# Moving the low parts of two weight sets from VectorE to GpSimd in a two-layer transformer kernel

## The chip, the cores and the metric

The kernel runs on one core of a Trainium2 chip. The metric is the device time of one execution in microseconds, as the median of several runs. The core's engines run side by side, each with an instruction stream of its own, and wait for each other by semaphores: TensorE (PE in the profile), VectorE (DVE), ScalarE (ACT), GpSimd (POOL) and SyncE (SP), which issues the transfers.

## What is computed

The input is x of 8 sequences x 512 rows x 256 columns. Two layers follow each other:

```python
xn = _layernorm(x)
x = x + _L0_attn_ref(xn, Wq, bq, Wk, bk, Wv, bv, Wo, bo)   # 16 heads of 64, rotary, causal softmax
      + _L0_ffn_ref(xn, weight_int8, weight_scale, bias)   # rows quantised to int8 by one scale
xn = _layernorm(x)
x = x + _L1_attn_ref(xn, compare_left, compare_right, threshold, gate_bias)
      + _L1_ffn_ref(xn, W_r, W_k, W_v, mu_r, mu_k)
```

The matrix products are to be nearly as precise as float32 ones, while TensorE multiplies float16. So each weight matrix is scaled by a power of two and split in a high part (float16 of the scaled weight) and a low part (float16 of what the high part leaves), and each product is made of three: high x high, high x low, low x high.

## The kernel before, in words

**Stages.** A short set-up loads x and the query and key weights and makes their high and low parts. The first layer, some 50 to 830 us of the span, handles 64 pairs of heads (8 sequences x 8 pairs). The second layer follows, one pass of `body3` per sequence.

**The passes.** Each engine has its own function `ring(n)`, called for n = -5 to 62. Pass n finishes pair n, computes scores and softmax of pair n+1 and projects queries and keys of phase n+5 (a phase is the queries or the keys of two pairs). Nothing is scheduled at run time: the order of the calls inside each `ring(n)` is the order in which that engine works, and each call waits for what it needs. The order around the change:

- TensorE: scores of (n+1, 0); `v(n)`; transposes `pt(n, j, h)` (L1773) of the probabilities of pair n, which for j = 0 wait until GpSimd has normalised them; from pass 10 on also the output projection `attended` (L1804) and the quantised layer `ffn`; `evens(n+5)`; scores of (n+1, 1); `odds(n+5)`; last `av(n)` (L1787).
- ScalarE: exponentials `exps(n+1, 0)` and, later in the pass, `exps(n+1, 1)` (L890), with copies and the high halves `high_e`, `high_o` of the rotated phase n+4 between them. `later_weights(n)` comes after all of them. It makes the high parts of the output weights, two quarters in pass 7 and two in pass 8 (L852, semaphore `wo_hi`), and those of the five matrices of the second layer in passes 24 to 28 (L808, `wr_hi`).
- VectorE: maxima of the scores of (n+1, 0) in three parts with `out_low(n-1)` (L1405) and `first_gap(n)` after the first; `second_gap(n)`; `even_terms(n+5)`; `inverse(n+1, 0)` (L1391), the reciprocals of the softmax sums; maxima of (n+1, 1); `odd_terms(n+5)`; `inverse(n+1, 1)`; `ring_end(n)`, in which `quantise` has its steps (L1415 to L1426).
- GpSimd: `normalise(n, 1)` (L646, four instructions, waits for `inverse(n, 1)`); `rotate(n+4)` (L618, L620); `low_e(n+4)` (L628), `low_o(n+4)` (L636), which wait for ScalarE's high halves; in some passes `add_bias` (L655); `normalise(n+1, 0)`; in some passes `add_ffn` (L662).

**Low parts.** VectorE makes each with one instruction, `scalar_tensor_tensor`: staged weight times `inv`, minus the high part. For the output weights (4 quarters of 128 x 512) that is `low_part(c)` in `ring_end` of passes 7, 8 and 10 (L1271). For the second layer (two of 128 x 256, three of 128 x 512) it is `weights_low` (L1219) in `first_gap` of passes 25 to 29.

**Who reads them.** `attended(0, 0, ...)` waits for `wo_lo` in passes 10 and 11. SyncE waits for `wo_lo` 4 before it loads the second layer's weights over the staged output weights. The second layer's products wait for `wr_lo` 5 after the last pass.

**Small steps.** The scales of the second layer's weights come from maxima over the whole matrices. `column_maximum` is in `first_gap(20)`; `weight_scale` (L1211 to L1213, three linked instructions of 1 to 5 columns) is in `second_gap(20)`, and three pairs of instructions on one to four columns (L1310 to L1318) are in `second_gap` of passes 21 to 23.

Of the kernel before, what the change touches and what calls it, by code (L numbers as in the profile page):

```python
# [6 lines left out]
SQ = 512  # L7
D = 256
# [19 lines left out]
NG = 9  # L28
# [15 lines left out]
def build(nc, x_d, weights_d, w8_d, bqk_d, vec_d, thr_d, gate_d, tab_d, out_d):  # L44
# [11 lines left out]
    with ctx:  # L56
# [205 lines left out]
        wr_hi = sem("wr_hi")  # L262
        wr_lo = sem("wr_lo")
        w8_done = sem("w8_done")
        xm_done = sem("xm_done")
# [315 lines left out]
        def _(pool):  # L581
# [75 lines left out]
            def add_ffn(b, h):  # L657
# [4 lines left out]
                pool.tensor_tensor(tiles, tiles, fft.rearrange("p (t d) -> p t d", t=2), ALU.add).then_inc(fx_done, 1)  # L662

            def ring(n):

# [5 lines left out]
                if b >= 0 and r % 4 == 1:  # L671
                    add_bias(b, r // 4)
                if n == NR - 2:
                    for h in range(2):
                        add_bias(NB - 1, h)
# [415 lines left out]
        def _(dve):  # L1091
# [174 lines left out]

            def low_part(c):

                part = slice(c * SQ, (c + 1) * SQ)
                dve.wait_ge(wo_hi, c + 1)  # L1270
                dve.scalar_tensor_tensor(out=wl[:, C_O:C_LR][:, part], in0=wst_r[:, part], scalar=inv[:, G_O:G_O + 1],  # L1271
                                         in1=wh[:, C_O:C_LR][:, part], op0=ALU.mult, op1=ALU.subtract).then_inc(wo_lo, 1)

            def part_maximum(c):
# [5 lines left out]
            def first_gap(n):  # L1280

                if n == 0:
                    roots(later_tiles, 1, (1, 2), wo)
                elif n == NB - 1:
                    dve.wait_ge(amax_done, NB)
                    dve.tensor_reduce(xmax1[:], amax[:], AX.X, ALU.max).then_inc(xm_done, 1)
                elif n == 20:
                    column_maximum(slice(G_L, NG), 4)
                elif 25 <= n < 25 + NG - G_L:
                    weights_low(G_L + n - 25, (wr_hi, n - 24), wr_lo)  # L1290

            def second_gap(n):
# [8 lines left out]
                elif 13 <= n < 17:  # L1301
# [3 lines left out]
                    else:  # L1305
                        weight_maximum(slice(G_WR + n - 14, G_WR + n - 13))
                elif n == 20:
                    weight_scale(slice(G_L, NG), 4)
                elif n == 21:
                    dve.scalar_tensor_tensor(out=sc_c[:], in0=sc[:, G_L:G_L + 1], scalar=D ** -0.5, in1=sc[:, G_R:G_R + 1],  # L1310
                                             op0=ALU.mult, op1=ALU.mult)
                    dve.tensor_scalar(sc_hr[:], sc[:, G_WR:G_WR + 1], 0.5, None, ALU.mult)
                elif n == 22:
                    link(dset, dve.tensor_tensor(thr_c[:], inv[:, G_L:G_L + 1], inv[:, G_R:G_R + 1], ALU.mult))
                    dve.scalar_tensor_tensor(out=thr_c[:], in0=thr_c[:], scalar=D ** 0.5, in1=thr[:], op0=ALU.mult, op1=ALU.mult)
                elif n == 23:
                    dve.tensor_scalar(sc_hv[:], sc[:, G_WV:G_WV + 1], 0.5, None, ALU.mult)
                    dve.tensor_scalar(omu[:], vec[:, V_MUR:V_MUR + 4], -1.0, 1.0, ALU.mult, ALU.add)  # L1318
                elif NR - 6 <= n <= NR - 3:
# [4 lines left out]
            def ring_end(n):  # L1324
# [3 lines left out]
                if n == 7:  # L1328
                    quantise(0, 0)
                    low_part(0)  # L1330
                elif n == 8:
                    input_scale()
                    low_part(1)
                elif n == 9:
                    for step in range(1, 4):
                        quantise(0, step)
                elif n == 10:
                    low_part(2)
                    low_part(3)

# [771 lines left out]
```

## Time and profile before

| | before |
|---|---|
| median of 3 runs | 1019.11 us (1018.42 to 1019.32) |
| the profiled execution | 1019.33 us, its span 1017.4 us |
| TensorE busy | 975.8 us (96%) |
| VectorE busy | 839.6 us (83%) |
| ScalarE busy | 746.0 us (73%) |
| GpSimd busy | 764.1 us (75%) |

The profile shows one execution. A line of the timeline gives the start in us, the time in us (of x instructions together, where it ends in a count), the engine, the line of the program, the operation, the tiles written and read, and in brackets how long the engine was idle before it and who ended that. A custom or pipelined instruction's end is modelled, so starts are surer than durations.

### The profile page before, as it was taken

To read this page: it belongs to the slowest core of one execution; us is meant where nothing else is said; L and a number is where in the kernel's file an instruction comes from. 1 tells how busy PE (TensorE), PEld (TensorE's weight loads), DVE (VectorE), ACT (ScalarE), POOL (GpSimd) and SP (SyncE) were. 2 spreads that over 40 slices of the span, in tenths; PEclk is the share of its full clock that TensorE was granted. 3 is DMA by queue.
4 is the path that set the end of the run, shared out by engine and by line. 5 is a ranking of instruction groups with operands and counts; after the bars stand their busy time and mean duration, and the time that the engine had idled before them with its cause. 6 is when DMAs were issued, how large, how long until landed. Compare 5 with 4: busy or idle time off the path is not lost.

```text
span 1017.4 us, 23654 instructions
## 1 busy us (share of the span) xinstructions
PE 975.8 (96%) x7956; PEld 673.2 (66%) x7956; DVE 839.6 (83%) x2272; ACT 746.0 (73%) x1998; POOL 764.1 (75%) x942
## 2 busy tenths in 40 slices
PE   5789999999999999999999999999999998989998
PEld 4556665766666666666666666666666675766776
DVE  7989999788889888887788777877878778999885
ACT  5989987667766677666767766667666776988984
POOL 3777768778778787878787878787878665878885
PEclk9999999999999999999999999999999999999999
DMA  8733535243433333333333333333333101111111
GB/s 271 242 111 119 155 121 160 79 131 112 124 111 93 105 106 94 95 114 96 93 95 119 96 103 97 116 97 100 105 96 95 53 1 27 35 35 35 48 55 43
DMA packets 102903, 101.32 MB, mean 100 GB/s; under 512 B 13952, under 2 KB 98560, under 8 KB 102144
## 3 DMA queue, kind: packets, MB, share of 16 engines
q1 hardware_dynamic: 102784, 99.81, 32.2%
q8 instruction: 65, 1.06, 0.5%
q14 instruction: 54, 0.44, 0.2%
HBM read 56.25 MB, written 40.90 MB: 95 GB/s over the span
## 4 chain that ended last, share of the span: by engine, by line
PE 70%; DVE 16%; ACT 4%; POOL 4%; issue 3%; DMA 2%; SPq 0%; DVEq 0%; POOLq 0%; ACTq 0%
PE bank L1690 23%; PE bank L1787 13%; PE bank L1773 12%; PE bank L1804 8%; PE bank L1761 6%; PE bank L1762 5%; DVE arena L1382 2%; POOL arena L646 2%; PE bank L1931 2%; DVE arena L1398 2%; ACT arena L890 1%; PE bank L1991 1%; DVE arena L1550 1%; DVE arena L1360 1%; DMA arena<-in_weights 1%
## 5 line engine op out<-in xcount | busy, mean ns | idle before, releaser
L646 POOL TENSOR_SCALAR arena<-arena,rc 128x128 f32<-128x128 f32 (+3 forms) x512 | 278.0, 560 | 176.5 <-DVE rc L1391 176.2
L890 ACT ACTIVATE arena<-arena,nm 128x256 f32<-128x256 f32 (+3 forms) x512 | 283.5, 554 | 109.0 <-DVE nm L1382 104.4
L1382 DVE CUSTOM_DVE_ANT_0 arena<-bank,mask_rows 128x256 f32<-128x256 f32 (+3 forms) x512 | 232.9, 483 | 89.0 <-PE bank L1762 83.9
L1773 PE MATMUL bank<-ident,arena 128*128 128x128 f32 x1280 | 211.8, 278 | 9.5 <-DVE arena L1398 4.4
L1773 PEld LDWEIGHTS bank<-ident,arena 128*128 128x128 f32 x1280 | 150.0, 141 | 68.4 <-DVE arena L1398 29.3
L1762 PE MATMUL bank<-arena 128*128 128x256 f16 (+3 forms) x512 | 152.9, 299 | 0.0
L1787 PE MATMUL bank<-arena 128*64 128x512 f32 (+3 forms) x1024 | 152.0, 439 | 0.0
L1761 PE MATMUL bank<-arena 128*128 128x256 f16 (+3 forms) x512 | 139.9, 300 | 2.0 <-DMA arena<-scr 2.0
L1787 PEld LDWEIGHTS bank<-arena 128*64 128x64 f32 x1024 | 67.8, 136 | 95.1 <-issue 70.6
L1398 DVE COPY arena<-bank 128x512 f32<-128x512 f32 (+3 forms) x256 | 124.5, 486 | 3.3 <-PE bank L1773 2.9
L898 ACT ACTIVATE arena<-bank 128x512 f32<-128x512 f32 (+3 forms) x256 | 108.3, 423 | 15.0 <-PE bank L1773 14.2
L1690 PE MATMUL bank<-xsh,wh 128*128 128x512 f16 x256 | 97.3, 380 | 3.1 <-DVE wl L1228 2.4
L1804 PE MATMUL bank<-wh,arena 128*128 128x256 f16 x512 | 99.7, 273 | 0.0
L1690 PE MATMUL bank<-xsl,wh 128*128 128x512 f16 x256 | 97.3, 380 | 0.0
L1690 PE MATMUL bank<-xsh,wl 128*128 128x512 f16 x256 | 97.3, 380 | 0.0
L890 ACT ACTIVATION_READ_ACCUMULATOR arena<-arena,nm 128x1 f32 x512 | 96.0, 187 | 0.0
L908 ACT ACTIVATE arena<-bank,bvs 128x512 f16<-128x512 f32 x64 | 44.0, 687 | 69.8 <-PE bank L1787 69.5
L1690 PE MATMUL bank<-wh,xsh 128*128 128x128 f16 x512 | 89.1, 219 | 1.6 <-DVE arena L1373 1.6
L1690 PE MATMUL bank<-wl,xsh 128*128 128x128 f16 x512 | 89.1, 219 | 0.0
L1690 PE MATMUL bank<-wh,xsl 128*128 128x128 f16 x512 | 89.1, 219 | 0.0
L618 POOL TENSOR_TENSOR arena<-arena 128x512 f32<-128x512 f32 x64 | 81.5, 1274 | 6.6 <-DVE arena L1373 6.5
L620 POOL TENSOR_TENSOR arena<-arena 128x512 f32<-128x512 f32 x64 | 83.0, 1296 | 0.0
(183 smaller groups left out, 2164.2 us busy)
## 6 DMA issues: line engine op xcount, KB each, us to landing
arena<-scr SPq DMA_DIRECT2D x320, 128.0 KB, 2.7
scr<-arena SPq DMA_DIRECT2D x256, 128.0 KB, 1.7
arena<-in_weights SPq DMA_DIRECT2D x5, 1024.0 KB, 7.5
x_sb<-in_x SPq DMA_DIRECT2D x8, 512.0 KB, 8.7
out<-x_sb SPq DMA_DIRECT2D x16, 256.0 KB, 2.2
xscr<-arena SPq DMA_DIRECT2D x12, 256.0 KB, 3.0
arena<-wh SPq DMA_DIRECT2D x40, 64.0 KB, 2.0
xsh<-xscr SPq DMA_DIRECT2D x6, 256.0 KB, 3.5
```

The lines of the kernel that those rows point to most:

```text
L620: pool.tensor_tensor(r_o, t_es, t_oc, ALU.add).then_inc(r1_done, 1)
L646: last = pool.tensor_scalar(pr[slot][:, OFF[i]:OFF[i + 1]], pr[slot][:, OFF[i]:OFF[i + 1]], rc[:, slot, i:i + 1], 1.0, ALU.mult, ALU.mult)
L890: act.activation(pr[slot][:, OFF[i]:OFF[i + 1]], pr[slot][:, OFF[i]:OFF[i + 1]], ACT.Exp, scale=-1.0, bias=nm[:, slot, i:i + 1], accum_out ...
L898: act.activation(ptf[h][:, TOFF[j]:TOFF[j + 1]], (pt0, pt1)[h][:, 0:P * (NT - j)], ACT.Copy).then_inc(ptf_done[h], 1)
L1382: dve.tensor_tensor_reduce(pr[slot][:, OFF[i]:OFF[i + 1]], s_tile[i], mask_rows[:, SQ - P * (i + 1):SQ], -1.0, -MASKED, ALU.add, ALU.min, ...
L1398: dve.tensor_copy(ptf[1][:, TOFF[j]:TOFF[j + 1]], pt1[:, 0:P * (NT - j)]).then_inc(ptf_done[1], 1)
L1690: last = pe.matmul(out, lhs, rhs, start=(a == 0), stop=(a == len(pairs) - 1))
L1761: pe.matmul(out, q, kd[par][:, hh, 0:(i + 1) * P], start=True, stop=False)
L1762: last = pe.matmul(out, q, kz[par][:, hh, 0:(i + 1) * P], start=False, stop=True)
L1773: last = pe.transpose(banks[5 + h][:, (i - j) * P:(i - j + 1) * P], pr[2 * par + h][:, OFF[i] + j * P:OFF[i] + (j + 1) * P], ident[:])
L1787: last = pe.matmul(ob[h * L:(h + 1) * L, j * P:SQ], vf[:, j, h * L:(h + 1) * L], ptf[h][:, TOFF[j]:TOFF[j + 1]], start=(j == 0), stop=(j = ...
L1804: last = pe.matmul(bank[:, t * D:(t + 1) * D], o[:, slot, rows], w[:, p, :], start=(p == 0 and a == 0 and t == 0), stop=(p == NP - 1 and a ...
```

## The change

The low parts move to GpSimd. There each takes two instructions: the staged weights are scaled in place, and behind a semaphore of their own the high part is subtracted. `later_low(n)` does it in `ring(n)` between `low_o`/`add_bias` and `normalise(n+1, 0)`: the output weights' four quarters in passes 7, 8, 9, 10, the second layer's five matrices in passes 26, 27, 28, 30, 31. VectorE's `low_part` and its part of `first_gap` go. Its small steps move from `second_gap` of passes 20 to 23 to `first_gap` of passes 21 to 24.

```diff
+            def low_part(w, staging, g, turn, high, done):
+                pool.wait_ge(*high)
+                pool.tensor_scalar(staging, staging, inv[:, g:g + 1], 1.0, ALU.mult, ALU.mult).then_inc(wst_scaled, 1)
+                pool.wait_ge(wst_scaled, turn + 1)
+                pool.tensor_tensor(w[1], staging, w[0], ALU.subtract).then_inc(done, 1)
+            def later_low(n):
+                if 7 <= n < 11:
+                    c = n - 7
+                    part = slice(c * SQ, (c + 1) * SQ)
+                    low_part([w[:, C_O:C_LR][:, part] for w in (wh, wl)], wst_r[:, part], G_O, c, (wo_hi, c + 1), wo_lo)
+                elif n in (26, 27, 28, 30, 31):
+                    c = (26, 27, 28, 30, 31).index(n)
+                    g = G_L + c
+                    low_part([wgroup(w, g) for w in (wh, wl)], staged(g), g, 4 + c, (wr_hi, c + 1), wr_lo)
...
                 if b >= 0 and r % 4 == 1:
                     add_bias(b, r // 4)
+                later_low(n)
...
-            def low_part(c):
-                part = slice(c * SQ, (c + 1) * SQ)
-                dve.wait_ge(wo_hi, c + 1)
-                dve.scalar_tensor_tensor(out=wl[:, C_O:C_LR][:, part], in0=wst_r[:, part], scalar=inv[:, G_O:G_O + 1],
-                                         in1=wh[:, C_O:C_LR][:, part], op0=ALU.mult, op1=ALU.subtract).then_inc(wo_lo, 1)
...
-                elif 25 <= n < 25 + NG - G_L:
-                    weights_low(G_L + n - 25, (wr_hi, n - 24), wr_lo)
+                elif n == 21:
+                    weight_scale(slice(G_L, NG), 4)
+                elif n == 22:
...
+                elif n == 23:
...
+                elif n == 24:
...
                 if n == 7:
                     quantise(0, 0)
-                    low_part(0)
                 elif n == 8:
                     input_scale()
-                    low_part(1)
...
-                elif n == 10:
-                    low_part(2)
-                    low_part(3)
```

The steps under `first_gap` 22, 23 and 24 are, unchanged, those that stood under `second_gap` 21 (`sc_c`, `sc_hr`), 22 (`thr_c`, two linked) and 23 (`sc_hv`, `omu`).

## Rows read from the trace of the kernel before

**Rows 1.** The page: busy time; costliest groups (busy, mean ns | idle before, releaser).

```profile
PE 975.8 (96%) x7956; PEld 673.2 (66%) x7956; DVE 839.6 (83%) x2272; ACT 746.0 (73%) x1998; POOL 764.1 (75%) x942
...
L646 POOL TENSOR_SCALAR arena<-arena,rc 128x128 f32<-128x128 f32 (+3 forms) x512 | 278.0, 560 | 176.5 <-DVE rc L1391 176.2
```

**Rows 2.** Timeline of TensorE: start of `av` in passes 19, 20, 24, 29, 30, 32.

```profile
303.49 0.65 PE L1787 MATMUL bank<-arena 128*64 128x512 f32 x2
...
316.46 0.65 PE L1787 MATMUL bank<-arena 128*64 128x512 f32 x2
...
366.22 0.65 PE L1787 MATMUL bank<-arena 128*64 128x512 f32 x2
...
429.35 0.65 PE L1787 MATMUL bank<-arena 128*64 128x512 f32 x2
...
441.54 0.65 PE L1787 MATMUL bank<-arena 128*64 128x512 f32 x2
...
466.24 0.65 PE L1787 MATMUL bank<-arena 128*64 128x512 f32 x2
```

**Rows 3.** Timeline of GpSimd, end of pass 7 and start of pass 8.

```profile
148.43 1.16 POOL L636 TENSOR_TENSOR arena<-arena 128x512 f16<-128x512 f32 x1 [0.38 <-ACT arena L873]
150.92 2.05 POOL L646 TENSOR_SCALAR arena<-arena,rc 128x128 f32<-128x128 f32 x4 [1.33 <-DVE rc L1391]
154.77 3.41 POOL L646 TENSOR_SCALAR arena<-arena,rc 128x128 f32<-128x128 f32 x4 [1.80 <-DVE rc L1391]
158.15 1.26 POOL L618 TENSOR_TENSOR arena<-arena 128x512 f32<-128x512 f32 x1
```

**Rows 4.** Timeline of ScalarE: high parts of the output weights in pass 7.

```profile
153.66 1.32 ACT L852 ACTIVATE wh<-arena,inv 128x512 f16<-128x512 f32 x2
```

**Rows 5.** Timeline of VectorE: `quantise` at the ends of passes 7 and 9.

```profile
154.49 1.20 DVE L1415 TENSOR_TENSOR arena<-xsh,xsl 128x1024 f32<-128x1024 f16 x1
...
179.00 0.72 DVE L1418 TENSOR_SCALAR arena<-arena,rscale 128x1024 f32<-128x1024 f32 x1
```

**Rows 6.** Timeline of TensorE: first transposes of pair 8, both heads.

```profile
156.56 0.61 PE L1773 MATMUL bank<-ident,arena 128*128 128x128 f32 x4
...
158.23 0.66 PE L1773 MATMUL bank<-ident,arena 128*128 128x128 f32 x4 [0.63 <-POOL arena L646]
```

**Rows 7.** Timeline of GpSimd: normalisations of pair 10.

```profile
175.68 2.05 POOL L646 TENSOR_SCALAR arena<-arena,rc 128x128 f32<-128x128 f32 x4
179.28 3.22 POOL L646 TENSOR_SCALAR arena<-arena,rc 128x128 f32<-128x128 f32 x4 [1.56 <-DVE rc L1391]
```

**Rows 8.** Timeline of GpSimd, second layer: a scale and the instruction that waits for it.

```profile
960.35 0.69 POOL L716 TENSOR_SCALAR arena<-arena,sc_hv 128x512 f32<-128x512 f32 x1
961.13 1.27 POOL L719 TENSOR_TENSOR x_sb<-x_sb,arena 128x512 f32<-128x512 f32 x1
```

**Rows 9.** Timeline of GpSimd: `normalise(29, 0)` in pass 28.

```profile
414.16 2.05 POOL L646 TENSOR_SCALAR arena<-arena,rc 128x128 f32<-128x128 f32 x4 [1.36 <-DVE rc L1391]
```

**Rows 10.** Timeline of VectorE: second step of `thr_c`, second gap of pass 22.

```profile
336.46 1.09 DVE L1315 SCALAR_TENSOR_TENSOR thr_c<-thr_c,thr 128x1 f32<-128x1 f32 x1
```

**Rows 11.** Timeline of VectorE and GpSimd: end of the first gap, pass 23.

```profile
346.18 0.29 DVE L1382 CUSTOM_DVE_ANT_0 arena<-bank,mask_rows 128x128 f32<-128x128 f32 x1 [1.06 <-PE bank L1762]
...
345.29 1.26 POOL L618 TENSOR_TENSOR arena<-arena 128x512 f32<-128x512 f32 x1
```

**Rows 12.** Timeline of TensorE: fill matmuls at two paces, an early stall.

```profile
16.17 4.02 PE L1667 MATMUL bank<-mask_rows,identb 128*128 128x128 bf16 x36
...
23.92 3.51 PE L1667 MATMUL bank<-mask_rows,identb 128*128 128x128 bf16 x60
...
45.99 0.27 PE L1761 MATMUL bank<-arena 128*128 128x256 f16 x1 [1.98 <-DMA arena<-scr]
```

**Rows 13.** The page: granted clock, tenths of full speed, in 40 slices.

```profile
PEclk9999999999999999999999999999999999999999
```

More of the change, by code:

```diff
@@ L263, in build @@
         wr_lo = sem("wr_lo")
+        wst_scaled = sem("wst_scaled")
         w8_done = sem("w8_done")
@@ L1288, in first_gap @@
                     column_maximum(slice(G_L, NG), 4)
-                elif 25 <= n < 25 + NG - G_L:
-                    weights_low(G_L + n - 25, (wr_hi, n - 24), wr_lo)
+                elif n == 21:
+                    weight_scale(slice(G_L, NG), 4)
+                elif n == 22:
+                    dve.scalar_tensor_tensor(out=sc_c[:], in0=sc[:, G_L:G_L + 1], scalar=D ** -0.5, in1=sc[:, G_R:G_R + 1],
+                                             op0=ALU.mult, op1=ALU.mult)
+                    dve.tensor_scalar(sc_hr[:], sc[:, G_WR:G_WR + 1], 0.5, None, ALU.mult)
+                elif n == 23:
+                    link(dset, dve.tensor_tensor(thr_c[:], inv[:, G_L:G_L + 1], inv[:, G_R:G_R + 1], ALU.mult))
+                    dve.scalar_tensor_tensor(out=thr_c[:], in0=thr_c[:], scalar=D ** 0.5, in1=thr[:], op0=ALU.mult, op1=ALU.mult)
+                elif n == 24:
+                    dve.tensor_scalar(sc_hv[:], sc[:, G_WV:G_WV + 1], 0.5, None, ALU.mult)
+                    dve.tensor_scalar(omu[:], vec[:, V_MUR:V_MUR + 4], -1.0, 1.0, ALU.mult, ALU.add)
             def second_gap(n):
@@ L1306, in second_gap @@
                         weight_maximum(slice(G_WR + n - 14, G_WR + n - 13))
[L1307 to L1318, printed above, removed]
                 elif NR - 6 <= n <= NR - 3:
```

## The prediction

> **What bounds the kernel now.** I began with the page's busy shares and its costliest groups [rows 1]. TensorE is busy 96% of the 1017.4 us span. GpSimd's normalisation group waits 176 us in all for VectorE's reciprocals. So GpSimd has time to give away, but only in those waits, and only time that TensorE loses or wins can move the end.
>
> TensorE's order is written out by hand, one pass of `ring(n)` per pair n, so a fixed group of its matmuls works as a clock for the passes. I took the first matmul of `av(n)` (L1787) in the timeline [rows 2]. The last three rows give the undisturbed pace: 429.35 to 441.54, pass 30, is 12.19 us; 441.54 to 466.24, passes 31 and 32, is 24.70, so pass 32 is 12.51 (the longer pass comes once in four, when n is a multiple of 4, with `ffn` in it). Against that pace:
> - passes 20 to 24, 303.49 to 366.22: 62.73 us where 2 x 12.51 + 3 x 12.19 = 61.59 would do. 1.14 us is lost, 0.46 of it in pass 20 (316.46 - 303.49 = 12.97 against 12.51). VectorE's small scale steps are in these passes.
> - passes 25 to 29, 366.22 to 429.35: 63.13 us against 12.51 + 4 x 12.19 = 61.27. 1.86 us is lost. VectorE's `weights_low` for the second layer is in these five.
>
> These two differences are prices in TensorE time, so they can be summed. They are also nearly all that the change can win there.
>
> **Part 1, second layer's low parts leave VectorE (passes 25 to 29).** Five `weights_low` go, and nothing replaces them on VectorE: -1.86 us. GpSimd gets two instructions each in passes 26, 27, 28, 30, 31. Price of a pair of 128x512: the scale by a column took 0.69 us and the dependent next instruction began 0.78 after its start [rows 8]; the f16 subtract took 1.16, as L636 shows [rows 3]. Together 1.94 us, the two 256-wide groups about 1.1. In its place, between `low_o` and `normalise(n+1, 0)`, GpSimd sat idle for 1.36 us [rows 9], so a 512-wide pair overruns by 0.6 us. `normalise(n+1, 0)` takes 2.05 us and TensorE does not use its result before the next pass; GpSimd waits again ahead of `normalise(n+1, 1)`. ScalarE's high parts are one to three passes ahead (24 to 28). The cover holds: 0. Part 1: **-1.86 us**, between -1.5 and -1.9.
>
> **Part 2, the small steps move half a pass.** `weight_scale` goes from the second gap of pass 20 to the first gap of 21, the three pairs of steps behind it from 21 to 23 into 22 to 24. Where they stand now they delay `even_terms`, on which TensorE waits. 
>
> In the first gap VectorE is idle for 1.06 us, until 346.18 in pass 23 [rows 11]. So the gap opens at 345.12. GpSimd is then in the last instruction of `normalise(n, 1)` and starts `rotate` (L618, 1.26 us) at 345.29. A step with one hold-up is served at that change-over, 0.2 us into the gap, and is free: so the `sc_c`/`sc_hr` and `sc_hv`/`omu` pairs. The `thr_c` pair is linked by a semaphore: its second step finds L618 started and waits for its end, 1.43 us into the gap, some 0.5 late with its own time. The price for TensorE lies between 0 and 0.5; I take 0.3. `weight_scale` has three linked steps. The first two should come through by the change-over, the third is a reciprocal of single columns; the pass's own reciprocals never look held up. If it is not held, 0.1; if it is, about 1. I take 0.1. Part 2: -1.14 + 0.3 + 0.1 = **-0.74 us**, between -1.14 and +0.3.
>
> The Trainium skill (SBUF — State Buffer, "Who interferes with whom") says that a VectorE instruction with two SBUF inputs shares a port pair with GpSimd and that the one that comes second fully blocks. The L1315 row agrees; by that rule a reciprocal with one input isn't held.
>
> **Part 3, output weights' low parts (passes 7 to 10).** Here the order matters. In GpSimd's `ring(7)` the new `low_part` stands between `low_o(11)` and `normalise(8, 0)` and waits for `wo_hi` 1. ScalarE makes that at the very end of its own `ring(7)`, behind all `exps(8, 1)`. GpSimd is not waiting for it today: it ends `low_o` at 148.43 + 1.16 = 149.59 and starts `normalise(8, 0)` at 150.92 [rows 3]. ScalarE starts the two high parts of that pass at 153.66, 1.32 us for both [rows 4]; the first is there at about 154.35. So this is a **new wait** of nearly 5 us, and queued behind it are `normalise(8, 0)`, `normalise(8, 1)`, `rotate(12)` and `low_e`/`low_o(12)`.
>
> Working forward: at 154.49 VectorE starts its `quantise` add with two SBUF inputs [rows 5], and today's `normalise(8, 1)` shows what that does to GpSimd: 3.41 us instead of 2.05. Whichever is first, the add or the scale, both are through at about 156.3 and the subtract ends near 157.5. Then 2.05 for `normalise(8, 0)` to 159.5 and 2.05 for `normalise(8, 1)` to 161.6. Today that second one ends at 158.18. TensorE needs the first at 156.56 and is already waiting for the second at 158.23 [rows 6]. It loses 161.6 - 158.2 = **+3.4 us**, in two stalls of 3.0 and then some 0.4 more than today. `rotate(12)` is as late, so ScalarE and VectorE are too, and nothing of it is won back later: every pass is paced from inside. With no hold-up at the port it would be 154.35 + 1.94 + 4.1 = 160.4, +2.2; with one more, +3.8. Taking VectorE's own four low parts out of passes 7, 8 and 10 gains nothing beyond this: VectorE's time there lies under the new stall or beside TensorE's work.
>
> In passes 8 and 10 the 1.94 us goes into waits that are long enough. In pass 9 `add_bias(0, 0)` stands there too, and GpSimd goes straight into `normalise(10, 0)` at 175.68 [rows 7]. Shifted by 1.9 it ends at 179.6, past 179.00, where VectorE's three `quantise` steps begin [rows 5]. Today's `normalise(10, 1)` beside them takes 3.22 us from 179.28; it begins 0.3 later and yields more often: +0.5 us, between 0 and 0.9, since `rotate(14)` right behind it is what ScalarE and then TensorE come to. Part 3: 3.4 + 0.5 = **+3.9 us**, between +2.2 and +4.7.
>
> SyncE's wait for `wo_lo` 4, ahead of the load of the second layer's weights, is met earlier than today (pass 10's place on GpSimd is before VectorE's), so the queue behind it isn't touched. `attended(0, 0, ...)` wants parts 1 and 2 in pass 10 and the rest in 11; they are there a pass before.
>
> **Sum.** 3.9 - 1.86 - 0.74 = **+1.3 us**. On the profiled execution's 1019.33 us that is 1020.6; it lies 0.2 above the median of the runs, so the forecast for the median is 1019.11 + 1.3 = **1020.4 us**. With all bounds at once: 2.2 - 1.9 - 1.14 = -0.8 to 4.7 - 1.5 + 0.3 = +3.5, so 1018.3 to 1022.6.
>
> **Rivals.**
> - *The stall costs TensorE's clock as well (slower).* The trace has no idle of 3 us while TensorE is at its upper level; after 1.98 us without work, up to 45.99, the matmuls ran on at full pace [rows 12]. What the lower level (1.2 GHz) costs is seen at the start: 36 fill matmuls in 4.02 us against 60 in 3.51 us later, 0.112 against 0.0585 each (the page's granted clock reads 9 in all slices [rows 13], so I go by the pace). There the stretch at half pace lasts from 16.17 for some 5.8 us, of which half is loss: +2.9. It decides if the 3.0 us stall at 156.56 is enough to drop the level. Then +1.3 + 2.9 = +4.2, 1023.3 us. The Trainium skill (TensorE: Matmul & The Clock Gate, "HAM oscillation — how this bites in real kernels") says that long idle gaps inside a kernel return the array to half rate. Against it: the stall is broken by four transposes and four score matmuls.
> - *Small steps are blocked in the first gap (slower).* For: L1315's 1.09 us. If the third step of `weight_scale` is held for `rotate`, +0.9, and `thr_c` costs its full 0.5: 1.3 + 0.9 + 0.2 = +2.4, 1021.5 us.
> - *The new wait is covered (faster).* The change is meant to use waits. If ScalarE's high part of pass 7 came before GpSimd's turn, part 3 would be 0 or even the removal of VectorE's share of the 3.41: -1.86 - 0.74 - 0.4 = -3.0, 1016.1 us. Against it stand the two clock times, 149.59 and 153.66.
>
> **Chances.** Forecast 0.64, first rival 0.09, second 0.14, third 0.06, other 0.07. About 0.2% (2 us) is what a measurement of this kernel tells from no change, so slower is above 1021.1, faster below 1017.1. The forecast case's own range, 1018.6 to 1022.2, puts some 0.08 above 1021.1; with 0.08 of the first rival, most of the second's 0.14 (its size is uncertain: 0.08) and half the unknown: slower 0.27, faster 0.06, same 0.67. Range for 8 in 10: 1018.4 to 1022.8.
>
> **What the changed profile should show.** GpSimd idle nearly 5 us in front of the first scale of `low_part`, released by ScalarE; TensorE stalls of 3.0 and about 1 us in front of L1773 for GpSimd's L646; 3.4 us more than today from `av(7)` to `av(8)`; `av(24)` to `av(29)` in 61.3; passes 20 to 24 in about 62.0. Wrong if `av(7)` to `av(8)` grows by under 2 us (then GpSimd's order isn't what I read), if passes 26 to 31 are longer than the pace (then GpSimd has no room), or if matmuls behind the stall run at half pace.

## The result and the profile after

The changed kernel takes 1021.87 us, the median of 8 executions (1020.68 to 1023.68), against 1019.18 (1017.99 to 1020.23) for the kernel before. The ratio is 1.0028, with a 95% interval of 1.0017 to 1.0038. It is slower by about 2.7 us. That is inside the range of 1018.4 to 1022.8 and 1.5 us above the forecast of 1020.4. The forecast called "no difference" the likeliest; by its own border of 1021.1 the result lies on the slower side, which it had given 0.27.

The profiled execution took 1023.2 us, with a span of 1020.9, and is one of the three slowest of the eight. The mean granted clock of all eight is below full: 0.995 in these three, 0.996, 0.997 and three times 0.998 in the others. In the profiled execution of the kernel before it is 1.00. The page of the kernel after, busy times and granted clock in 40 slices:

```profile
PE 978.0 (96%) x7956; PEld 675.5 (66%) x7956; DVE 829.9 (81%) x2263; ACT 747.3 (73%) x1998; POOL 775.5 (76%) x960
...
PEclk9999998999999999999999999999999999999999
...
L647 POOL TENSOR_SCALAR arena<-arena,rc 128x128 f32<-128x128 f32 (+3 forms) x512 | 275.2, 556 | 162.2 <-DVE rc L1397 161.4
```

Against [rows 1], VectorE gave away 9.7 us and GpSimd took on 11.4; GpSimd's waits for the reciprocals fell from 176 to 162 us. So the work moved as meant, into waits that were there. TensorE is busy 2.2 us longer with the same 7956 matmuls, and one slice of the granted clock, the seventh (153 to 179 us), has an 8 where [rows 13] has only 9. The two belong together.

I measure with the same clock marks as in the prediction, the first matmul of `av(n)` (now L1793). Timeline of TensorE, kernel after, starts of `av` in passes 7, 19 and 29:

```profile
152.39 2.38 PE L1793 MATMUL bank<-arena 128*64 128x512 f32 x16
...
308.88 2.37 PE L1793 MATMUL bank<-arena 128*64 128x512 f32 x16
...
431.97 2.38 PE L1793 MATMUL bank<-arena 128*64 128x512 f32 x16
```

From these marks in both traces, the length of each pass (`av(n-1)` to `av(n)`) that differs by more than 0.03 us:

| pass | before | after | difference |
|---|---|---|---|
| 8 | 12.76 | 18.48 | +5.72 |
| 10 | 13.78 | 13.85 | +0.07 |
| 11 | 14.08 | 13.98 | -0.10 |
| 20 | 12.97 | 12.61 | -0.36 |
| 22 | 12.57 | 12.19 | -0.38 |
| 23 | 12.49 | 12.33 | -0.16 |
| 25 to 29 | 63.13 | 61.26 | -1.87 |
| 58 | 12.87 | 12.94 | +0.07 |

The sum is +2.99. The execution began 0.3 us ahead of the one before, so `av(63)` starts at 843.41 instead of 840.75, 2.66 later. All of the loss up to there is in pass 8. In the second layer this one execution loses 0.8 us more, which is taken up at the end. The lengths of passes are compared and not their starts, because the set-up ahead of them varies by itself: `av(0)` starts at 65.2 to 67.0 us in the twelve traces.

Timeline of GpSimd, kernel after, end of pass 7 and start of pass 8 (compare [rows 3]):

```profile
148.13 1.16 POOL L637 TENSOR_TENSOR arena<-arena 128x512 f16<-128x512 f32 x1 [0.38 <-ACT arena L893]
154.16 1.78 POOL L668 TENSOR_SCALAR arena<-arena,inv 128x512 f32<-128x512 f32 x1 [4.88 <-ACT wh L872]
156.03 1.16 POOL L670 TENSOR_TENSOR wl<-arena,wh 128x512 f16<-128x512 f32 x1
157.16 4.08 POOL L647 TENSOR_SCALAR arena<-arena,rc 128x128 f32<-128x128 f32 x8
161.20 1.27 POOL L619 TENSOR_TENSOR arena<-arena 128x512 f32<-128x512 f32 x1
```

GpSimd stands still for 4.88 us in front of the new scale, until ScalarE's high part comes. The scale takes 1.78 us and not 0.69, since VectorE's `quantise` add runs from 154.19 for 1.19 us beside it. Then both normalisations of pair 8 follow at once (x8, 4.08 us), and `rotate(12)` starts at 161.20 instead of 158.15. TensorE at the same place, kernel after (compare [rows 6]):

```profile
159.26 0.66 PE L1779 MATMUL bank<-ident,arena 128*128 128x128 f32 x4 [2.84 <-POOL arena L647]
...
161.29 1.11 PE L1779 MATMUL bank<-ident,arena 128*128 128x128 f32 x4 [0.80 <-POOL arena L647]
...
164.33 0.63 PE L1696 MATMUL bank<-xsh,wh 128*128 128x512 f16 x1
...
169.48 0.38 PE L1696 MATMUL bank<-xsh,wh 128*128 128x512 f16 x1
```

Two stalls, 2.84 and 0.80 us. Behind the second the same four transposes take 1.11 us instead of 0.66, and a projection matmul 0.63 instead of 0.38. The stretches of that time, kernel after (duration, then busy time of TensorE, its weight loads, VectorE, ScalarE and GpSimd, the granted clock, DMA share and GB/s); the kernel before has 1.00 for the clock in all of them:

```profile
156.00:159.00 3.00, 0.42 (x8) 0.25 (x5) 0.39 (x1) 0.96 (x3) 2.97 (x5) 1.00 0.89 241
159.00:162.00 3.00, 1.94 (x12) 1.41 (x13) 0.78 (x4) 0.60 (x1) 3.00 (x6) 0.68 0.87 292
162.00:165.00 3.00, 3.00 (x12) 2.04 (x12) 1.82 (x4) 2.50 (x8) 3.00 (x4) 0.50 0.33 117
165.00:168.00 3.00, 3.00 (x15) 1.48 (x14) 1.83 (x4) 1.10 (x4) 2.76 (x3) 0.68 0.40 131
168.00:171.00 3.00, 2.43 (x14) 1.02 (x14) 2.77 (x13) 1.62 (x7) 2.05 (x4) 1.00 0.33 102
```

TensorE ran at its lower level (1.2 GHz, half of 2.4) for (0.32 + 0.50 + 0.32) x 3.00 / 0.5 = 6.8 us after the stall, fully busy in nearly all of it. In stretches of 0.5 us the clock begins to fall between 160.0 and 160.5, while TensorE does the short work between the two stalls, and is back between 166.5 and 167.0. That is what the first rival of the prediction describes. The question for the experiments was whether the 5.72 us really splits into a stall and a loss by the clock, and whether the wait causes both.

### The profile page after: what moved, and what is told of

Same layout as the page of the kernel before. It is cut to its first block, busy times and chain, and to the rows that moved or that the text cites. A ratio compares the mean times of both kernels' runs of the same rounds, so it can differ in the third digit from the quotient of the medians.

```text
span 1020.9 us, 23664 instructions
## 1 busy us (share of the span) xinstructions
PE 978.0 (96%) x7956; PEld 675.5 (66%) x7956; DVE 829.9 (81%) x2263; ACT 747.3 (73%) x1998; POOL 775.5 (76%) x960
## 4 chain that ended last, share of the span: by engine, by line
PE 73%; DVE 12%; ACT 5%; POOL 5%; issue 3%; DMA 1%; SPq 0%; DVEq 0%; POOLq 0%; ACTq 0%
PE bank L1696 24%; PE bank L1793 13%; PE bank L1779 12%; PE bank L1810 8%; PE bank L1767 6%; PE bank L1768 6%; PE bank L1937 2%; POOL arena L647 2%; DVE arena L1388 2%; ACT arena L910 1%; PE bank L1997 1%; DVE arena L1404 1%; DMA arena<-in_weights 1%; DVE x_sb L1578 1%; DVE arena L1556 1%
## 5 line engine op out<-in xcount | busy, mean ns | idle before, releaser
L647 POOL TENSOR_SCALAR arena<-arena,rc 128x128 f32<-128x128 f32 (+3 forms) x512 | 275.2, 556 | 162.2 <-DVE rc L1397 161.4
L1793 PE MATMUL bank<-arena 128*64 128x512 f32 (+3 forms) x1024 | 151.9, 439 | 0.0
L1793 PEld LDWEIGHTS bank<-arena 128*64 128x64 f32 x1024 | 67.8, 136 | 95.0 <-issue 70.6
L619 POOL TENSOR_TENSOR arena<-arena 128x512 f32<-128x512 f32 x64 | 81.6, 1276 | 5.5 <-DVE arena L1379 5.4
```

What stands on the lines that cost most here:

```text
L647: last = pool.tensor_scalar(pr[slot][:, OFF[i]:OFF[i + 1]], pr[slot][:, OFF[i]:OFF[i + 1]], rc[:, slot, i:i + 1], 1.0, ALU.mult, ALU.mult)
L1793: last = pe.matmul(ob[h * L:(h + 1) * L, j * P:SQ], vf[:, j, h * L:(h + 1) * L], ptf[h][:, TOFF[j]:TOFF[j + 1]], start=(j == 0), stop=(j = ...
```

## The experiments

My theory was that the new wait on GpSimd costs a stall of some 3.4 us, and the clock's fall behind it a further 2.3. The rival was that the clock's fall only goes with the stall, so that TensorE would have been as late without it; another, that GpSimd's additional work and not its wait makes the delay. "Pass 8" is `av(7)` to `av(8)`, read from the trace of each run. The median of the kernel before was 1019.26 us beside runs 1 to 4, and 1018.93 beside runs 5 to 8 and beside runs 9 and 10.

**1. The same stall, filled.** TensorE runs useless matmuls in place of the wait, so that it stays active; nothing else is changed from the kernel after.

```diff
                 v(n)
+                if n == NP:
+                    pe.wait_ge(ptf_done[1], 4 * n)
+                    fill(46)
                 pt(n, 0, 0, o)
```

> The changed kernel, with 46 fill matmuls (2.7 us of work without use) on TensorE in pass 8, between v(8) and the first transposes, where it stands idle for 2.84 us. Theory A (GpSimd's new wait costs 3.4 us by itself, and the drop of TensorE's clock that it sets off another 2.3): the granted clock stays at 1.0 over the stall, av(7) to av(8) takes 12.76 + 3.4 = 16.2 us instead of 18.48, and the median is 2.3 us under that of the changed kernel, near 1019.6. Theory B (all 5.7 us come from the wait and what is queued behind it; the slow matmuls lie beside other engines' work): the clock may stay up, but pass 8 still takes 18.2 to 18.5 us and the median stays near 1021.9.

Measured: 1020.40 us, ratio 1.0013 (1.0004 to 1.0023); pass 8 took 16.13 us, 3.37 more than before. Timeline of TensorE, stall filled:

```profile
160.76 0.66 PE L1779 MATMUL bank<-ident,arena 128*128 128x128 f32 x4 [0.29 <-POOL arena L647]
...
162.79 0.66 PE L1779 MATMUL bank<-ident,arena 128*128 128x128 f32 x4 [0.94 <-POOL arena L647]
```

Both groups of transposes take 0.66 us, and the granted clock is 1.00 in all stretches from 153 to 168. GpSimd is as late as in the kernel after (this execution's `av(0)` is 1.46 us later, its second transposes 1.50), so the stall costs 3.37 by itself, and the clock the other 18.48 - 16.13 = 2.35 us in the profiled execution. The median came down by 1.5 us, not by the 2.3 that was expected. Two things on record fit that. Four of the ten executions still had a clock of 0.998 or less; the profiled one, the slowest of them, has half-clock time in the set-up and near 866 us (clock 0.66 from 865 to 870). And the 2.35 us were measured in an execution of the kernel after with a clock of 0.995, which only three of its eight have. The six executions of this run at 0.999 or 1.00 have a median of 1020.24 us, so an estimate of what the clock costs the median execution of the kernel after is 1021.87 - 1020.24 = 1.6 us (the kernel before had 1019.18 and 1019.26 beside the two).

**2. ScalarE's high parts a pass earlier.** The wait goes, because what it waits for is there.

```diff
-                elif n in (7, 8):
+                elif n in (6, 7):
                     act.wait_ge(setup_done, 3)
-                    for c in (2 * n - 14, 2 * n - 13):
+                    for c in (2 * n - 12, 2 * n - 11):
```

> The changed kernel, with ScalarE's high parts of the output weights one pass earlier (two quarters in pass 6, two in pass 7). GpSimd's order and work are those of the change; only what it waits for in pass 7 is there before. Theory A (the wait is the cost, not the work moved): no idle of GpSimd before its first scale, no stall of TensorE over 1 us in pass 8, av(7) to av(8) at 12.2 to 12.8 us, up to 0.3 us more in pass 6 or 7 for ScalarE's earlier work; the median lands at 1019.2 - 3.0 = 1016.2, between 1015.6 and 1016.8. Theory B (GpSimd has no room for two more instructions in passes 7 to 10, wait or not): pass 8 stays above 14 us, the median above 1018.

Measured: 1016.88 us, ratio 0.9974 (0.9964 to 0.9985). Pass 8 is 12.19, below the 12.76 of before. Pass 7 grew by 0.48, more than the 0.3 that was allowed for; only ScalarE's 1.33 us of high parts, now at 141.56, are new there, so they are the likely price. The median is just above the expected 1015.6 to 1016.8. Timeline of GpSimd, high parts early:

```profile
148.74 1.17 POOL L637 TENSOR_TENSOR arena<-arena 128x512 f16<-128x512 f32 x1 [0.85 <-ACT arena L893]
149.89 0.70 POOL L668 TENSOR_SCALAR arena<-arena,inv 128x512 f32<-128x512 f32 x1
150.68 1.16 POOL L670 TENSOR_TENSOR wl<-arena,wh 128x512 f16<-128x512 f32 x1
151.81 2.06 POOL L647 TENSOR_SCALAR arena<-arena,rc 128x128 f32<-128x128 f32 x4
```

The same two instructions, now 0.70 and 1.16 us, cost nothing where their input is ready. So it was the wait and not the work.

**3. Only the output weights' part of the change.** The kernel before, with the four low parts of the output weights on GpSimd (passes 7 to 10) and all else left alone.

```diff
+            def later_low(n):
+
+                if 7 <= n < 11:
+                    c = n - 7
...
-                    low_part(0)
                 elif n == 8:
                     input_scale()
-                    low_part(1)
...
-                elif n == 10:
-                    low_part(2)
-                    low_part(3)
```

> The kernel before, with the output weights' low parts alone moved to GpSimd as in the change (passes 7 to 10). The second layer's low parts and the small steps stay with VectorE at their old places. Theory A (the parts add): pass 8 takes 18.5 us, passes 20 to 29 are exactly those of before, and the median is 1019.2 + 5.6 = 1024.8, between 1024.0 and 1025.6. Theory C (the parts lean on each other, the gain of one needs the other): it lies outside that.

Measured: 1024.67 us, ratio 1.0052 (1.0035 to 1.0069): this part alone costs about twice what the whole change does. The median is as expected; pass 8 is not. It took 16.47 us where 18.5 was expected: the first stall is the same (2.85 us), but the stretch at half clock was half as long, and no second stall is seen. Passes 20 to 29 are those of before to 0.03 us. So executions with the same first stall can lose different amounts by the clock. Stretches of this kernel (same columns as above):

```profile
159.00:162.00 3.00, 1.11 (x6) 1.05 (x7) 0.00 (x0) 0.00 (x0) 3.00 (x7) 0.79 0.89 239
162.00:165.00 3.00, 2.93 (x16) 1.73 (x14) 1.70 (x6) 1.46 (x4) 3.00 (x4) 0.64 0.73 264
165.00:168.00 3.00, 3.00 (x21) 1.83 (x21) 2.73 (x6) 2.62 (x9) 3.00 (x4) 1.00 0.40 131
```

That is (0.21 + 0.36) x 3.00 / 0.5 = 3.4 us at the lower level. The four executions of this run had clocks of 0.993, 0.997, 0.998 and 0.998; the profiled one is the fastest of them.

**4. Only the second layer's part and the small steps.** The kernel before with parts 1 and 2 of the prediction.

```diff
+                if n in (26, 27, 28, 30, 31):
+                    c = (26, 27, 28, 30, 31).index(n)
+                    g = G_L + c
+                    low_part([wgroup(w, g) for w in (wh, wl)], staged(g), g, c, (wr_hi, c + 1), wr_lo)
...
-                elif 25 <= n < 25 + NG - G_L:
-                    weights_low(G_L + n - 25, (wr_hi, n - 24), wr_lo)
+                elif n == 21:
+                    weight_scale(slice(G_L, NG), 4)
```

> The kernel before, with the other two parts of the change: the second layer's low parts on GpSimd, the small steps in the first gaps; VectorE keeps the output weights' low parts. Theory A (the parts add): passes 7 to 11 are exactly those of before, passes 20 to 24 take 0.9 us less and passes 25 to 29 1.87 us less, so 1019.2 - 2.8 = 1016.4, between 1015.7 and 1017.1. Theory C as before: the gain is less than 2 or more than 3.5 us.

Measured: 1017.88 us, ratio 0.998 (0.997 to 0.999). The passes came as expected: 25 to 29 lose 1.86 us, 20, 22 and 23 lose 0.36, 0.38 and 0.14, passes 7 to 11 are untouched (pass 21 was 0.21 longer, in this run alone), and `av(63)` comes 2.59 earlier. The median gained only 1.4, a miss. A part of what is missing lies behind TensorE's end. In the profiled execution (clock 0.999) the last matmuls start 2.60 us earlier than before (1008.15 against 1010.75), but the span is only 1.8 shorter. VectorE's last additions, four in a row until 1014.76 in the kernel before, stop in the middle for GpSimd here, which makes up 0.35 us; the other 0.45 comes after VectorE's last instruction. Second layer's part only, the end of TensorE and VectorE:

```profile
1008.15 2.78 PE L2005 MATMUL bank<-arena 128*128 128x256 f16 x24
...
1011.63 0.88 DVE L1586 SCALAR_TENSOR_TENSOR x_sb<-bank,arena,x_sb 128x256 f32<-128x256 f32 x2 [0.44 <-POOL x_sb L735]
```

Another part can be the clock: five of the ten executions had 0.998 or less, and the other five have a median of 1017.22, 0.7 below that of all ten. The medians of runs 3 and 4 do not add (+5.4 and -1.4, against +2.7 for the whole change), the lengths of the passes do, but for pass 8.

**5. Each quarter of the output weights where its input is long there.** The kernel after, with the four low parts in passes 8, 9, 10 and, behind `rotate(15)`, 11.

```diff
-                if 7 <= n < 11:
-                    c = n - 7
+                if 8 <= n < 11 or n == 11 and turned:
+                    c = n - 8
...
                 rotate(n + AHEAD - 1)
+                if n == 11:
+                    later_low(n, True)
                 low_e(n + AHEAD - 1)
```

> The changed kernel, with GpSimd's four low parts of the output weights one pass later (8, 9, 10 and, behind rotate(15), pass 11); ScalarE's high parts stay in passes 7 and 8. Theory A (the cost is the wait of pass 7): GpSimd never waits for the high parts, pass 7 takes its 12.36 us, pass 8 some 12.2 us (the half microsecond that high_early showed too, because VectorE's first low part no longer holds normalise(8, 1)), passes 9 to 12 as in the changed kernel: av(7) to av(12) shorter than before by 0.6 us, the median at 1019.2 - 3.3 = 1015.9, between 1015.2 and 1016.7. Theory B (no room on GpSimd in pass 11, since ScalarE waits for low_e and low_o there or TensorE for the last quarter): pass 11 or 12 grows by 0.5 to 2 us.

Measured: 1015.98 us (1015.44 to 1016.32), ratio 0.9970 (0.9959 to 0.9981). It beats both kernels: 3.0 us below the one before, and 5.9 below the median of the change. All seven executions had the full clock. Timeline of GpSimd, late quarters:

```profile
150.94 2.06 POOL L647 TENSOR_SCALAR arena<-arena,rc 128x128 f32<-128x128 f32 x4 [1.32 <-DVE rc L1399]
154.81 2.84 POOL L647 TENSOR_SCALAR arena<-arena,rc 128x128 f32<-128x128 f32 x4 [1.80 <-DVE rc L1399]
157.61 1.27 POOL L619 TENSOR_TENSOR arena<-arena 128x512 f32<-128x512 f32 x1
...
162.33 0.69 POOL L668 TENSOR_SCALAR arena<-arena,inv 128x512 f32<-128x512 f32 x1
163.10 1.16 POOL L670 TENSOR_TENSOR wl<-arena,wh 128x512 f16<-128x512 f32 x1
```

`normalise(8, 1)` takes 2.84 us where it took 3.41 [rows 3], because VectorE's `low_part(0)` no longer runs beside it: with that the stall of 0.63 us in [rows 6] goes, and pass 8 is 12.19. In pass 11, where the last quarter now stands, nothing was lost against the kernel after (13.98 in both).

**6. The first quarter one step later.** Its low part stands behind `normalise(8, 0)`, so that less is queued behind the wait.

```diff
                 normalise(n + 1, 0, (n + 1) % 2)
+                if n == 7:
+                    part = slice(0, SQ)
+                    low_part([w[:, C_O:C_LR][:, part] for w in (wh, wl)], wst_r[:, part], G_O, 0, (wo_hi, 1), wo_lo)
```

> The changed kernel, with the first quarter's low part one call later in pass 7, behind normalise(8, 0). GpSimd waits for ScalarE just as long as in the change, but only normalise(8, 1) and what follows are queued behind. Theory A (the price of a wait is what is queued behind it): the low part ends at the same time, 3.0 us before normalise(8, 0) would have let TensorE go on; normalise(8, 1) is 1.35 us later than before, TensorE's one stall stays about 2 us, the clock stays up, pass 8 takes 12.76 + 1.35 = 14.1 us, and the median is 1019.2 + 1.35 - 2.8 = 1017.8, between 1017.0 and 1018.6. Theory B (the wait itself costs, wherever it stands): pass 8 takes 16 to 18.5 us.

Measured: pass 8 took 14.10, 1.34 more than before, as expected; the median was 1019.76 us, ratio 1.0008 (0.9999 to 1.0018), a miss by 1.2 us. Timeline of TensorE, first quarter one step later:

```profile
156.21 0.61 PE L1782 MATMUL bank<-ident,arena 128*128 128x128 f32 x4
...
159.23 0.66 PE L1782 MATMUL bank<-ident,arena 128*128 128x128 f32 x4 [1.98 <-POOL arena L647]
```

In this execution the clock stayed up behind the stall of 1.98 us. Its only half-clock time in the layers lies near 862 us (clock 0.72 from 860 to 865). But nine of the ten executions had a mean clock of 0.998 or less, against 4 of 16 for the kernel before beside them. That raised a question of its own, for run 9: does a stall of 2 us already make a loss of clock more likely?

**7 and 8. One and two more pairs a pass on GpSimd.** The kernel before, with useless pairs of a scale and a subtract of 128x512 in each of passes 32 to 55, to measure how much room GpSimd has.

```diff
+                if 32 <= n < 56:
+                    for _ in range(1):
+                        load()
```

(`range(2)` in the second; `load()` is the scale, the wait for it and the subtract.)

> The kernel before, with a useless pair of GpSimd instructions on 128x512 (scale, then subtract, 1.94 us) in each of the passes 32 to 55, at the place of the change's low parts. Theory A (room on GpSimd is given by its waits for the reciprocals, 1.2 to 1.4 us and 1.8 to 2.3 us in a pass, and by next to nothing in the passes with add_bias and add_ffn, n = 33, 37, ... 53): 18 passes stay at 12.19 or 12.51 us; the other six, or the ones after them, grow by about 1.3 us each, 8 us in all, so some 1027 us, between 1023 and 1031. Theory B (a share of 75% busy leaves 3 us in every pass): nothing changes, 1019.

Measured: 1024.78 us in the one execution taken, 5.5 above the profiled execution of the kernel before (1019.33). Eighteen of the 24 passes are unchanged to 0.02 us. Passes 34, 42 and 50 grew by 0.25 each and 38, 46 and 54 by 1.43: 5.04 together. That is less than the 8 us expected. The call of `ring` on GpSimd ahead of each of them (33, 37, 41 and so on) holds an `add_bias` (L656) and an `add_ffn` (L663) as well. Timeline of GpSimd, one more pair, in `ring(37)` and the start of `ring(38)`:

```profile
524.94 1.28 POOL L656 TENSOR_TENSOR x_sb<-x_sb,fbow 128x512 f32<-128x512 f32 x1
...
526.98 1.17 POOL L674 TENSOR_TENSOR arena<-arena,wh 128x512 f16<-128x512 f32 x1
528.11 2.51 POOL L647 TENSOR_SCALAR arena<-arena,rc 128x128 f32<-128x128 f32 x4
530.59 1.27 POOL L663 TENSOR_TENSOR x_sb<-x_sb,arena 128x512 f32<-128x512 f32 x1
531.84 2.06 POOL L647 TENSOR_SCALAR arena<-arena,rc 128x128 f32<-128x128 f32 x4
533.87 1.27 POOL L619 TENSOR_TENSOR arena<-arena 128x512 f32<-128x512 f32 x1
```

No idle time is left in front of any of them, and TensorE waits 1.21 us for the second normalisation at 533.95. Why every other of the six costs 0.25 only, I did not follow up.

> As one_more_pair, with two such pairs (3.9 us) in each pass. Theory A: in the 18 passes without add_bias the pairs exceed the two waits by 0.5 to 0.7 us, which the 0.9 us between the end of normalise(n+1, 1) and TensorE's need for it still covers, so they grow by 0 to 0.3 us; the other six grow by 3.3 us each: 20 to 25 us in all, 1039 to 1044. Theory B (GpSimd's time just adds once it is full, 3.9 - 3.0 in each pass): all 24 grow alike, by 0.9 us, 1041 us; the sums are near, the passes tell.

Measured: 1053.52 us. Neither expectation (1039 to 1044, or 1041) came near. The loss is not spread evenly: it sits where the first one had it, but is larger. Passes 34, 38, 42, 46, 50 and 54 grew by 4.3 to 5.0 us, three others by 0.92, three by some 0.65, the rest by 0.03 at most. Behind each of the six long stalls stands a stretch at half clock. Stretches of the kernel with two more pairs:

```profile
480.00:487.00 7.00, 4.79 (x51) 3.28 (x48) 4.43 (x18) 2.72 (x7) 6.92 (x12) 1.00 0.13 29
487.00:490.50 3.50, 3.50 (x17) 2.60 (x16) 1.39 (x3) 2.26 (x7) 3.50 (x4) 0.52 0.11 37
490.50:494.00 3.50, 3.50 (x28) 2.42 (x26) 2.48 (x7) 1.53 (x5) 3.32 (x4) 1.00 0.34 112
```

So one pair (1.94 us) is free in most passes and costs where the two additions stand beside it; a second pair isn't free, and its long stalls are followed by the clock's fall. Both runs are single executions. The change puts one pair into a pass. Of its nine passes only 9 has `add_bias` and only 10 `add_ffn`, none has both.

**9. Run 6 with its stall filled.** Useless matmuls again.

```diff
+                if n == NP:
+                    pe.wait_ge(ptf_done[1], 4 * n)
+                    fill(30)
                 pt(n, 0, 1, o)
```

> one_call_later, with 30 fill matmuls (1.8 us of work without use) on TensorE in its remaining stall of pass 8, ahead of the second head's first transposes. one_call_later's profiled execution kept its clock in pass 8 and gave 1018.15 us, but most of its other executions show a granted clock of 0.995 to 0.998 and its median was 1019.76, not 1017.8. Theory A (in those executions the 2 us stall of pass 8 lowered the clock): with the fills nearly all executions are back at 0.999 to 1.0, and the median is 1017.8, between 1017.2 and 1018.5; pass 8 stays at 14.1 us. Theory D (the clock drops elsewhere, by chance, as in the kernel before): the clocks and the median stay as in one_call_later, near 1019.7.

Measured: 1018.36 us, ratio 0.9994 (0.9985 to 1.0003), with pass 8 unchanged at 14.10. Four of ten executions had a clock of 0.998, the others more: fewer than the nine of run 6, but not "nearly all back" as expected, and against 4 of 21 for the kernel before beside them. The passes are as long as in run 6 and the median is 1.4 us lower. That points to the clock as what run 6 missed, by a fall behind the 2 us stall in many of its executions. It isn't seen directly: only the profiled execution of each run has a trace, and there the clock held in pass 8 in both.

**10. `thr_c` in two passes.** Run 5, with the second step in the first gap of pass 25.

```diff
                     link(dset, dve.tensor_tensor(thr_c[:], inv[:, G_L:G_L + 1], inv[:, G_R:G_R + 1], ALU.mult))
-                    dve.scalar_tensor_tensor(out=thr_c[:], in0=thr_c[:], scalar=D ** 0.5, in1=thr[:], op0=ALU.mult, op1=ALU.mult)
...
+                elif n == 25:
+                    dve.scalar_tensor_tensor(out=thr_c[:], in0=thr_c[:], scalar=D ** 0.5, in1=thr[:], op0=ALU.mult, op1=ALU.mult)
```

> late_quarters, with the second of the two linked thr_c steps in the first gap of pass 25 instead of 23. Theory A (the 0.15 us by which pass 23 is still too long come from this step, which finds GpSimd's L619 started): av(22) to av(23) takes 12.19 us, pass 25 stays at 12.19, since the step is served at the change-over and is short; the median is 0.15 us under late_quarters, 1015.8, beyond what the runs can tell. Theory B (any step in the first gap costs, wherever it is): the 0.15 us move to pass 25. Against the kernel before both give a ratio of 0.997, and this is the version to keep if it holds.

Measured: pass 23 took 12.18 instead of 12.33 to 12.35, and pass 25 stayed at 12.19. So the linked second step is what costs 0.15 us in pass 23, and alone it is free. The median, 1016.64 us (ratio 0.9978, 0.9969 to 0.9987), is not below run 5's; 0.15 us is less than such a comparison resolves. Four of its eleven executions had a clock of 0.998 and none of run 5's seven, with passes 1 to 22 alike, so a part of run 5's lead is luck.

## Why the prediction was right, and where it wasn't

The range held, and the new wait cost what it was said to cost. But the loss is twice the forecast one, and one of the prediction's own signs of being wrong came true: matmuls behind the stall ran at half pace. That the time stayed in the range is luck in part, since errors on the other side took up some of the clock's cost.

- **What bounds the kernel.** Right. The marks at `av(n)` put every effect into its pass, and the passes not named in the table agree to 0.03 us.
- **Part 1**, forecast -1.86, measured -1.87, and -1.86 alone in run 4. The cover holds. A 128x512 pair took 0.69 and 1.16 us on GpSimd, a 128x256 one 0.48 and 0.67, and all were free in passes 26 to 31.
- **Part 2**, forecast -0.74, measured -0.90. The term that was mis-sized is `thr_c`, 0.15 (run 10) against 0.3; `weight_scale`, taken at 0.1, was free: its reciprocal took 0.19 us, and the step before it 0.63. Of the 1.14 us that could be won at most, 0.10 stayed in pass 20 (12.61 against 12.51), which the sum had taken as won. The second step of `thr_c` was held, as expected, until GpSimd's L619 was over: VectorE, kernel after, pass 23:

```profile
349.68 0.29 DVE L1309 TENSOR_TENSOR thr_c<-inv 128x1 f32<-128x1 f32 x1
350.01 1.21 DVE L1310 SCALAR_TENSOR_TENSOR thr_c<-thr_c,thr 128x1 f32<-128x1 f32 x1
```

  GpSimd's instruction ran from 349.94 to 351.21; the step before it, also on one column per partition, took 0.29, so nearly all of the 1.21 us is waiting. The Trainium skill (SBUF — State Buffer, "Who interferes with whom") says that a VectorE instruction with two SBUF inputs contends with a GpSimd instruction that reads SBUF, and that the pair of ports they share is an exclusive lock. The trace agrees, with these numbers.
- **Part 3, the stall in pass 8**, forecast +3.4, measured +3.37 with the clock kept up (run 1). Its steps came out within some 0.2 us: a wait of 4.88 (nearly 5), both normalisations through at 161.24 in an execution that runs 0.3 ahead (161.6), stalls of 2.84 and 0.80 (3.0 and about 1). Run 2 shows the cause: the same instructions at the same place, without the wait, cost TensorE nothing in pass 8. One reading was off without harm: the 3.41 us of today's `normalise(8, 1)` was put down to the `quantise` add alone, but 0.57 of it was VectorE's `low_part(0)` (2.84 without it in run 5). Nor were the waits in passes 8 and 10 long enough by themselves: in the kernel before, GpSimd waits 0.51 and 0.56 us there in front of the normalisation of the first head, and the pair of 1.94 us is taken up only by the wait in front of the second.
- **Part 3, pass 10**, forecast +0.5, measured +0.07, and -0.10 in pass 11. The step that failed is the shift of 1.9 us. VectorE's `low_part(1)` had run beside `normalise(9, 1)`; with it gone that takes 2.08 us instead of 2.51, so GpSimd came to pass 9 0.4 us earlier than the sum had it. Both normalisations of pair 10 still run into the three `quantise` steps, 5.38 us in one go, but `rotate(14)` starts at 187.96, against 187.89, which is the 182.47 of the kernel before plus the 5.42 us by which pass 8 had ended later. The working took the removed VectorE instructions as a gain of nothing; one of them was holding GpSimd. Timeline of GpSimd, kernel after, pass 9:

```profile
172.68 2.08 POOL L647 TENSOR_SCALAR arena<-arena,rc 128x128 f32<-128x128 f32 x4 [1.81 <-DVE rc L1397]
...
182.61 5.38 POOL L647 TENSOR_SCALAR arena<-arena,rc 128x128 f32<-128x128 f32 x8
187.96 1.27 POOL L619 TENSOR_TENSOR arena<-arena 128x512 f32<-128x512 f32 x1
```

- **The term that was left out, the clock.** +2.35 us in the profiled execution, some 1.6 in the median one by the estimate of run 1; no execution of the eight had the full clock. It stood in the text as the first rival, with 2.9 and a chance of 0.09. Its size was near; its chance was too low. The reason against it was that four transposes and four score matmuls break the stall. They are short: TensorE is busy for some 1.2 us between the two waits, and the clock fell during that work, at about 160.1 (0.68 in the mean of 159 to 162). I had also taken the stall of 1.98 us [rows 12], which left the pace alone, as a bound. Run 6's 1.98 us stall left it alone too in the profiled execution, yet nine of its ten executions had a mean clock of 0.998 or less. One row that shows a thing not happening says little about something that happens in some executions and not in others. The sentence of the Trainium skill in the rival (TensorE: Matmul & The Clock Gate, "HAM oscillation — how this bites in real kernels") was right here, by the 0.50 in the stretch from 162 to 165.
- **The sum.** With the measured terms, the last one being pass 58, whose cause stays open: 3.37 + 2.35 + 0.07 - 0.10 - 1.87 - 0.90 + 0.07 = +2.99; less the 0.3 by which this execution began early, +2.69, against the 2.66 by which `av(63)` is late. That the medians differ by 2.69 too is chance. The two profiled executions differ by 1023.2 - 1019.33 = 3.87 us: 2.66 up to `av(63)`, 0.84 in the second layer, and 0.37 outside the span, a term that the sum does not have. The time outside the span is 2.26 us in the median of the eight executions and 1.96 for the kernel before; it is 2.2 to 2.3 in all other runs built on the whole change and 1.9 to 2.0 in runs 3 and 4, and why stays open. The forecast's +1.3 misses the clock (2.35 in the profiled execution), and errs in passes 10 and 11 (0.5) and part 2 (0.16) on the other side.
- **The other rivals.** Blocked small steps: not seen, passes 20 to 24 took 61.83 us, forecast about 62.0. A covered wait: not in this change, but run 5 gets nearly what that rival was priced at, 1016.0 against 1016.1 us, by moving the quarters behind their inputs.

## What to carry to other kernels

Work that fits into an engine's idle time is only free where its own input is ready: look up the end of the producer and the start of the new consumer on the two timelines, and if there is a gap, price all that is queued behind it. The amount of idle time on the engine (here 176 us) says nothing about this; the same work 0.3% above or 0.3% below the kernel before differed only in which pass it stood in. And when a forecast stall of TensorE is about 2 us or more, put the clock's fall into the sum, not among the rivals: no execution with the stall of 2.84 us had the full clock, and in the profiled one the price of this stall rose from 3.37 to 5.72 us.

## What the runs showed of the hardware

- A stall of 2.84 us, 1.2 us of short matmuls and one more of 0.80 brought 6.8 us at 1.2 GHz in one execution; the same stall in run 3 brought 3.4 us. In the first the clock fell 0.9 us after TensorE had begun again, in run 3 just before it did (between 160.5 and 161.0; the stall ends at 160.88). Six stalls in run 8 were each followed by some 3.4 us at half clock. The loss by a stall is therefore not one number: here 2.35 us in one execution, and in run 3, where pass 8 grew by 3.71 in all, only 0.34 if the stall was worth 3.37 there too.
- A VectorE instruction that is taken away can speed up GpSimd: four normalisations took 3.41 us beside the `quantise` add and `low_part(0)`, 2.84 beside the add alone, and 2.05 alone; in pass 9, 2.51 beside `low_part(1)` and 2.08 without it.
- Every kernel has a place near 862 us, at the start of the second layer (near 897 in run 8), where TensorE waits 1.20 and then 0.63 us, and behind that place the clock fell in five of the twelve traces and held in seven. Stretches of the kernel before, where it holds, and then of the kernel after, where it falls:

```profile
865.00:870.00 5.00, 4.91 (x41) 3.87 (x40) 4.66 (x13) 4.90 (x12) 4.06 (x3) 1.00 0.00 0
```

```profile
865.00:870.00 5.00, 4.37 (x23) 2.80 (x22) 4.48 (x6) 4.22 (x9) 2.57 (x3) 0.66 0.11 27
```

  It goes with most of the 0.8 us that the profiled execution of the kernel after loses in the second layer (TensorE is 1.2 us later there than in the kernel before by its next long wait, counted from `av(63)`), and falls like this one can make single executions of one kernel differ by more than many edits are worth. Lengths of passes, which repeat to 0.02 us, showed effects of 0.1 us that no median did.
- A pass of run 3 and the kernel after differ by 2 us at the same code and the same stall. What decides between the two lengths of the stretch at half clock stays open; no run here was made for it.
